# Scores of two tiles moved to other PSUM banks, constants after the key split, and a planner with longer path lengths and an urgency per stage

## What is computed

```python
x = x + _L0_xattn_ref(_layernorm(x), ctx_512, ctx_512)          # 32 query heads on 8 key heads, 64 keys, head size 8
x = x + _L0_ffn_ref(_layernorm(x), w_router, w_fc, w_proj)      # 2 experts of 1024, one of them taken for each row
x = x + _L1_xattn_ref(_layernorm(x), ctx_512, Wq, Wkv_expand, Wout)   # 16 heads of 16, causal, projected out
x = x + _L1_ffn_ref(_layernorm(x), ...)                          # 8 gelu experts of 128..512, two taken, plus a shared one
```

## Time and profile before

| | us |
|---|---|
| median of 3 runs (416.74 to 418.52) | 417.0 |
| the profiled execution | 420.97 |
| its span | 419.2 |
| TensorE busy in it | 373.0 |
| VectorE, ScalarE, GpSimd busy | 235.2, 221.3, 93.3 |

### The profile page before, as it was taken

The page is one execution under the profiler, slowest core; times in us unless marked ns, Lnnn a source line. Parts: engine busy times, 40 slices in busy tenths (PEclk is TensorE's granted clock), DMA queues, the critical chain, the costliest instruction groups (busy, mean ns, idle before and its releaser), DMA issues.

```text
span 419.2 us, 9361 instructions
## 1 busy us (share of the span) xinstructions
PE 373.0 (89%) x3768; PEld 302.9 (72%) x3768; DVE 235.2 (56%) x611; ACT 221.3 (53%) x419; POOL 93.3 (22%) x173
## 2 busy tenths in 40 slices
PE   3355939999999999997999999899998999996896
PEld 1343838888888877987778888588876888775574
DVE  4798494869587447788344212855348036436242
ACT  2344832654654555595684312667644236775662
POOL 7872112322123032310001334000053120002000
PEclk9975776999999999997999999699999999999699
DMA  9990000000000000000000000000000000000000
GB/s 190 410 396 11 2 0 2 2 2 2 2 2 0 3 2 2 2 2 0 2 3 27 2 0 1 2 1 2 14 16 1 2 0 2 3 2 25 0 2 26
DMA packets 8218, 12.16 MB, mean 29 GB/s; under 512 B 4464, under 2 KB 6768, under 8 KB 7408
## 3 DMA queue, kind: packets, MB, share of 16 engines
q1 hardware_dynamic: 8176, 11.57, 8.3%
HBM read 10.52 MB, written 1.05 MB: 28 GB/s over the span
## 4 chain that ended last, share of the span: by engine, by line
PE 73%; DVE 16%; ACT 5%; issue 3%; POOL 2%; POOLq 0%; DVEq 0%; ACTq 0%
PE Y L1226 23%; PE H L1226 22%; PE S L1226 15%; PE S L1267 4%; PE S L1327 3%; PE S L1291 1%; PE S L1234 1%; DVE PT L990 1%; DVE MN L989 1%; ACT A L778 1%; PE S L1243 1%; PE S L1392 1%; ACT L778 1%; DVE K L976 1%; DVE KT L1057 1%
## 5 line engine op out<-in xcount | busy, mean ns | idle before, releaser
L1226 PE MATMUL H<-XT,WF 128*128 128x256 f32 x256 | 62.5, 395 | 0.0
L869 POOL TENSOR_TENSOR A<-R 128x512 f32<-128x512 f32 x32 | 33.3, 1039 | 125.8 <-PE Y L1226 74.9
L1226 PE MATMUL Y<-WP,A 128*128 128x256 f32 x256 | 59.5, 382 | 0.0
L1226 PE MATMUL H<-GH,W 128*128 128x256 f32 x168 | 50.6, 407 | 7.1 <-ACT GH L769 4.2
L778 ACT ACTIVATE A<-H,B 128x256 f32<-128x256 f32 x84 | 38.9, 475 | 32.1 <-PE Y L1226 22.7
L1226 PEld LDWEIGHTS H<-XT,WF 128*128 128x128 f32 x256 | 49.0, 198 | 8.4 <-ACT R L752 0.8
L1226 PEld LDWEIGHTS Y<-WP,A 128*128 128x128 f32 x256 | 47.3, 190 | 6.1
L1226 PE MATMUL Y<-A,W 128*128 128x256 f32 x168 | 50.5, 397 | 0.2 <-ACT A L778 0.2
L752 ACT ACTIVATE R<-H 128x512 f32<-128x512 f32 x32 | 19.1, 597 | 46.2 <-PE H L1226 46.1
L1226 PEld LDWEIGHTS H<-GH,W 128*128 128x128 f32 x168 | 30.7, 199 | 14.4 <-ACT A L778 5.9
L1180 DVE TENSOR_TENSOR YG<-YS,Y 128x256 f32<-128x256 f32 x32 | 13.4, 420 | 39.1 <-ACT YS L795 39.0
(11 more groups left out here) (183 smaller groups left out, 647.1 us busy)
## 6 DMA issues: line engine op xcount, KB each, us to landing
W<-in_w SPq DMA_DIRECT2D x2, 1344.0 KB, 11.0
WF<-in_wf SPq DMA_DIRECT2D x2, 1024.0 KB, 7.8
WP<-in_wp SPq DMA_DIRECT2D x2, 1024.0 KB, 9.8
X<-in_x SPq DMA_DIRECT2D x8, 128.0 KB, 8.4
out_dram<-X SPq DMA_DIRECT2D x8, 128.0 KB, 1.7
CD<-in_ctx_in SPq DMA_DIRECT2D x2, 256.0 KB, 5.4
C<-in_ctx_in SPq DMA_DIRECT2D x1, 256.0 KB, 2.9
CT<-in_ctxT SPq DMA_DIRECT2D x1, 256.0 KB, 3.9
```

The costliest lines, as they stand in the source:

```text
L869: nc.gpsimd.tensor_tensor(flat(A0[:, n % 2, :, :]), R0[:, n % 2, :], R0[:, n % 2, :], ALU.mult).then_inc(a0_ready, 1)
L1226: return nc.tensor.matmul(o, a, b, start=start, stop=stop, skip_group_check=shared)
```

## The change

It changes five things.

1. `ring_of` takes the place of `FILLS` where a bank is claimed: scores 0 and 1 of tiles 0 and 1 in `attn0` go to ring H, scores 2 and 3 to ring Y. All others stay in S.
2. The constants `m` and `g` need the key split of tile 1 first, so they stand behind it on GpSimd.
3. The path length of a step also runs through block i + 1 of its stage.
4. The urgency has a pair for each stage (51 pairs) instead of thirteen for kinds of steps; `SWITCH` goes from 5.3 to 132.3, `CHANGE` from 8.0 to 96.3, and `SLACK` from 0.039, 0.052, 0.154, 0.024 to 0, 0.15, 0.17, 0.36 (TensorE, ScalarE, VectorE, GpSimd).
5. ScalarE's copy of the turned rows of `ffn1` waits, from group 1 on, for its own gelu of the group before.

```diff
+def ring_of(s):
+
+    if (s[0], s[2]) == ("attn0", "s") and s[1] < 2:
+        return "HY"[s[3] // 2]
+    return FILLS.get((s[0], s[2]))
...
-SWITCH = 5.3
-CHANGE = 8.0
-SLACK = {"pe": 0.039, "act": 0.052, "dve": 0.154, "pool": 0.024}
+SWITCH = 132.3
+CHANGE = 96.3
+SLACK = {"pe": 0, "act": 0.15, "dve": 0.17, "pool": 0.36}
...
-URGENCY = {"attn0": (38.7, 20.0), "attn1": (-9.9, 32.6), "attn1_keys": (-23.0, -18.9),
-           "ffn0": (-33.7, 4.9), "ffn0_body": (-114.2, -4.5), "ffn1": (669.6, -114.4), "ffn1_body": (-36.9, 30.7),
-           "zero": (-347.7, 19.6), "constg": (-587.6, 61.3), "constm": (64.6, -29.8), "consti": (-58.3, 210.5)}
+URGENCY = {
+    "const": "i -378.3 96  m -496.4 -98.4  g -218.5 409.5  ",
+    "attn0": "c -255.1 191.6  v -55.9 167.4  ln -816.8 168  q 469.2 361.9  k 192.6 478.1  s 381.1 440  "
+             "e 576.7 205.1  b -86 311  p 111.8 318.8  o 7 690.5  n -330.4 219.7  ",
+    "attn1": "kv 344.6 232.9  k -165.7 -573.8  v -318.8 280.5  ln 699.3 528.8  x 2455 -394.3  "
+             "w -552.7 297  q 372.7 -377.1  s -472.5 -312.6  m 1316.6 212.4  p 273.8 -370.2  "
+             "o 410.5 -281.1  n 486.8 403  a 162.3 -263.6  r -624.9 -264.2  ",
+    "ffn0": "v 342.3 -236.6  ln 293.5 552.7  x 717.3 354.8  r 1270.1 243.6  g -1398.8 -26  "
+            "u -1056.3 54.3  d -349.5 323.5  y 31.6 -149.8  ",
+    "ffn1": "v 66.7 -385.4  ln 139.5 -210.9  x 555.9 -379.6  i 909.9 -262.4  r 32 -308.4  "
+            "e -715.9 181.4  t 610.1 167.2  d -85.7 11.9  g 421.8 -856.7  c 9.7 312.5  w 547.6 -1012  "
+            "y 1391.9 93.8  o -267.7 -153.8  b 651.8 -428.1  z 324.2 666.3  "}
...
     for name in "img":
-        add(("const", 0, name, 0))
+        add(("const", 0, name, 0), *[("attn0", 1, "c", 0)] * (name != "i"))
...
             if k + 1 < len(work):
                 ways.append(way_to_end(s, k + 1))
+            later = s[:3] + (s[3] + 1,)
+            if later in known and k < len(work_of(later)):
+                ways.append(way_to_end(later, k))
...
-        base, step = URGENCY[kind]
+        g = s[1] if s[0][0] == "f" else s[1] // 2
+        base, step = URGENCY[s[0]][s[2]]
...
-                b = FILLS[c[0], c[2]]
+                b = ring_of(c)
...
-            h |= evacuate("ffn1", "x", lambda g, i: flat(XT1[:, :, :]), lambda b, i: b[:, :])
+            def turned_rows1(g, _):
+                b, done = filled(act, "ffn1", g, "x", 0)
+                if g:
+
+                    act.wait_ge(gx_ready, g)
+                nc.scalar.copy(flat(XT1[:, :, :]), b[:, :]).then_inc(done, 1)
```

More of the change, by code:

```diff
@@ L85 @@
 MODE_CHANGE = 0.09
-SWITCH = 5.3
-CHANGE = 8.0
-SLACK = {"pe": 0.039, "act": 0.052, "dve": 0.154, "pool": 0.024}
+SWITCH = 132.3
+CHANGE = 96.3
+SLACK = {"pe": 0, "act": 0.15, "dve": 0.17, "pool": 0.36}
 GELU = {("ffn1", s) for s in "bdc"}
 EXP = {("attn0", "e"), ("attn1", "p"), ("ffn0", "g"), ("ffn1", "e"), ("ffn1", "t")}
-BODY = {("ffn0", "u"), ("ffn0", "d"), ("ffn0", "y"), ("ffn1", "c"), ("ffn1", "w"), ("ffn1", "y"), ("ffn1", "o")}
-URGENCY = {"attn0": (38.7, 20.0), "attn1": (-9.9, 32.6), "attn1_keys": (-23.0, -18.9),
-           "ffn0": (-33.7, 4.9), "ffn0_body": (-114.2, -4.5), "ffn1": (669.6, -114.4), "ffn1_body": (-36.9, 30.7),
-           "zero": (-347.7, 19.6), "constg": (-587.6, 61.3), "constm": (64.6, -29.8), "consti": (-58.3, 210.5)}
+URGENCY = {
[11 rows of a table added]
+URGENCY = {part: {w[0]: (float(w[1]), float(w[2])) for w in zip(*[iter(text.split())] * 3)} for part, text in URGENCY.items()}
 BODIES = [("ffn0", 0)] + [x for g in range(GROUPS - 1) for x in (("ffn0", g + 1), ("ffn1", g))] + [("ffn1", GROUPS - 1)]
@@ L264, in make_orders @@
     steps, needs = steps_and_needs()
-    follow = {}
+    known, follow = set(steps), {}
     for p, firsts in needs.items():
@@ L355, in make_orders @@
             for c in claims(s):
-                used[FILLS[c[0], c[2]]].append(c)
+                used[ring_of(c)].append(c)
         free[e] = done[s, k] = at + d
@@ L502, in mixed_network @@
             for c in claims(step):
-                turn[c] = len(order[FILLS[c[0], c[2]]])
-                order[FILLS[c[0], c[2]]].append(c)
+                turn[c] = len(order[ring_of(c)])
+                order[ring_of(c)].append(c)
         for r in READERS:
             for step in orders[r]:
-                b = FILLS.get((step[0], step[2]))
+                b = ring_of(step)
                 if b and reader(step) == r:
@@ L799, in _ @@
                      ("ffn0", "g"): exps("ffn0", E0), ("ffn0", "u"): leaky, ("ffn1", "e"): exps("ffn1", E1),
-                     ("ffn1", "t"): top_exp, ("ffn1", "b"): gelu_biases, ("ffn1", "d"): inner,
+                     ("ffn1", "t"): top_exp, ("ffn1", "b"): gelu_biases, ("ffn1", "d"): inner, ("ffn1", "x"): turned_rows1,
                      ("ffn1", "c"): hidden, ("ffn1", "y"): expert})
```

## The result

The changed kernel takes **390.5 us** (median of 4 runs, 389.08 to 391.18) against 417.1 (median of 4, 416.74 to 418.52). The ratio is 0.935, with a 95% interval of 0.9315 to 0.9389. That is 26.6 us less, where the prediction had 16. Of these 30.0 some 3 us belong to the execution that was profiled before and not to the change: it ran at a mean granted clock of 0.935, while others of the same kernel had spans of 414.3 us at 0.967 and 415.4 at 0.947. At nearly equal clock the gain is still 27 us (414.3 at 0.967 against 387.1 at 0.969).

The account below looks back on a forecast made before the run. It took TensorE, busy 373.0 of 419.2 us, as the bound, its idle time mostly at the start. 421.0 - 15 (start) - 1 (middle and end) = 405.0; the profiled execution stood 4.0 above the median, so 401, range 388 to 415.

Parts of the forecast that it names:

- the rival of a better order behind the start: Behind the start: 5 to 10 us more late idle time goes; 386 to 395 us, chance 0.20.
- Constants behind the key split: GpSimd at the start: masks' 5.5 us leave the front, first queries start 4 to 5 us earlier.
- Banks: Scores of tiles 0 and 1 in H and Y: TensorE's 3.47 us wait at 19.14 goes.
- The hand-made start: Start worked out from durations: last score of tile 1 at 27.4, first u at 46 us, bounds 42 and 58.
- What of it reaches the end: Start: of 20 us, 5 return as TensorE work left for later; gain 15 us, bounds 3 and 21.
- The middle and the end: Idle time of 6.6 + 10.7 us behind the start: 1 us of gain, between +6 and -6.
- Table loads: ScalarE's loads in the last group's gate chain: most stay; one saved there would give 1.3 us.
- The added wait in ScalarE's copy: ScalarE's copy waits for its own earlier gelu: three waits of 0 to 0.1 us, taken as zero.
- The rival of a start only partly shorter: Start: first u at 50 to 58, VectorE having other steps ahead; gain 3 to 10, 407 to 414 us, chance 0.18.
- The slower rival: Behind the first body: TensorE starved at three later bodies, 23 us in all; 419 to 428 us, chance 0.13.
- What would show it: Signs in the trace: first H product at 42 to 50 us, TensorE busy 360 to 375, idle about 30.

Follow-up runs that it names:

- masks_first: Changed kernel with only GpSimd's list edited: masks built right behind the identity, as in the kernel before; 394.5 us.
- gates_later: Changed kernel with only GpSimd's list edited: rows for the gates built behind the masks instead of right behind the key split of tile 1; 388.8 us.
- ring_off_replan: Changed kernel with scores of tiles 0 and 1 back in ring S and the lists planned anew; 398.2 us.
- early_v2: Changed kernel, start lists edited: gate rows later, tile 1 keys and scores earlier, turned rows, router and first two u ahead of zero-row products; 395.1 us.
- z_later: Lists of gates_later with turned rows, router and first two u of group 0 moved ahead of the zero-row products; 399.2 us.
- all_but_urgency: Changed kernel with the thirteen old urgencies, everything else as changed; 446.9 us, ratio 1.069 to the kernel before.

## Why the prediction was right, and where it was off

The direction and the place of the first gain were right, and 390.5 lies in the range, 2.5 us from its lower end. The forecast of 401 was 10.5 us too high, and the time lies outside the 395 to 407 around it. It fell in the range of the rival of a better order behind the start (386 to 395, chance 0.20). That it is inside the stated range is in part luck: the gain behind the start, 17.5 us, is far above the 6 that the range allowed it, and the start stayed far below its upper bound of 21. By its steps:

- *Constants behind the key split.* Power at 4.65 (said: about 5), queries 0 from 5.91 (they started after variance 1, as said), split 0 until 8.0 (8.2), keys copied at 9.24 to 10.65 (9.4 to 10.8). masks_first measures the masks' part at 4.0 us of the whole. But the step took both constants to lie beside work that doesn't wait for them. The gate rows cost queries 1 2.8 us, and gates_later's median is 1.7 lower, which is not clear of noise. The 2 us that the prediction feared for slower key splits did not come on GpSimd: the splits took 2.8 and 1.8 us where 3.1 were taken. VectorE was the engine that waited.
- *Banks.* Right that the wait goes, too small in size: 3.5 us of wait in the earlier trace rows, 7.7 us in ring_off_replan, since the new order would wait 6.73 at one score alone.
- *The hand-made start.* Said first score 13.3, last of tile 1 27.4, first H product 46; measured 16.78, 35.5, 56.90, at the worse of the two bounds (58). Of the 8 us by which the last score was late, 3 are the slowed queries, and 5 lie between the scores of tile 0 and tile 1: TensorE waited 5.38 us for a bank until VectorE had subtracted two `kv` results, then did the transposes of tile 0's probabilities and only behind them the keys of tile 1, and VectorE waited 2.96 us for these. The hand-made order left that wait out. The chain behind the last score took 21.4 instead of 18.6, with the copies KT, queries of tile 2 and zero-row products in it.
- *What of it reaches the end.* Said 15 us; the lost time of the start fell by 12.4. Two errors met here. The mark moved by 9 instead of 20, but by that mark TensorE had done 24.3 us of work and not 5 less than before (20.9). The price of the start came out nearly right with the wrong working, which is luck. The start must be priced by lost time, not by when the first body begins: early_v2 and z_later moved the mark another 12.5 and 8.3 us ahead and were slower.
- *The middle and the end.* This is the term that was mis-sized: +1 us against 14.5 + 3.0 = 17.5. I had counted TensorE's idle time, 6.6 us in the middle, as all there was. 21.2 us were lost there, most of it as slow or waiting matmuls that count as busy. The page had it before the prediction: the granted clock in the earlier trace rows dips to 7 and 6 tenths in the middle, and an engine busy at such a clock isn't a full one. In the first seven slices it stands at 5 to 7 tenths in five, where the prediction read four. And the rival of a better order behind the start, at 0.20, described it too narrowly, as recovered idle time at the end, which gave 3.0 us; it had the time right and the place wrong.
- *Table loads.* I expected most to stay, since `SWITCH` only acts within 0.15 us. 26 fell to 18, as the attention went away from the gelu bodies. The urgencies don't do this alone: there are 24 loads with the old path lengths and 20 with the old constants. All kernels that keep the changed urgencies, path lengths and the three constants throughout have 18.
- *The added wait in ScalarE's copy* was taken as nothing, and the trace after agrees: what idle time stands before its four executions, 2.9 us in all, was ended by TensorE's transposes and not by ScalarE's own gelu.
- *The rival of a start only partly shorter* had its condition met, the first `u` between 50 and 58 (56.90), and its price of 3 to 10 us, without the gain of the middle, missed: 407 to 414.
- *The slower rival* did not come. Its mechanism, TensorE starved of the next tiles behind an early body while VectorE works in order, shows in early_v2, which is 4.6 us slower than the changed kernel. all_but_urgency is slower by 29.8 us than the kernel before, but with a late start and a crowded gelu body, which is not this mechanism.
- *What would show it.* TensorE's idle time fell to 32.7 (said about 30). Its busy time, 356.5, fell below the 360 to 375 that I gave, for the same reason as above. First score, last score, the rows XN (48.54, said 36 to 42) and the first H product (56.90, said 42 to 50) missed their windows.

## What to carry over

Price an order of work by what the busiest engine loses in each stretch, at full-clock cost, and not by idle time or by when some milestone comes. Hold the lost time against the granted clock of the stretch, since one execution differs from the next in it. Parts of a plan that are good together can each be a loss alone, so a part's worth says little without the others. Where engines run in order, moving a read ahead on one engine moves everything behind it; look at what that engine then waits for.

## What the hardware showed

GpSimd slowed VectorE in some pairs of instructions and not in others. Beside GpSimd's selection of 128x1024 bfloat16 (1.23 us each), VectorE's copies and two-input operations from SBUF took 1.19 to 1.48 us instead of 0.43 to 0.56 (after against gates_later); each was so held for 0.8 to 0.9 us, less than one GpSimd instruction. The Trainium skill, SBUF — State Buffer, section "Who interferes with whom", has this as an exclusive lock by order of issue, and these rows agree. In the changed kernel VectorE read its scores from PSUM at 0.68 to 0.69 us beside the selections of the masks (32x1024 bfloat16) from 19.38 to 21.79, the same as elsewhere.

All table loads of these traces last 1.28 us. The 2.7 us that the prediction quotes are, in the Trainium skill, ScalarE: Activation LUTs, section "What ACT_TABLE_LOAD costs", the load together with a drain. That section gives the load alone as about 1.28 us, so trace and page agree on it.
